# Row maxima of the attention scores: 1024 columns at a time from the operands that lie on all 128 rows

## The chip, the core and the metric

The kernel runs on one core of one Trainium2 chip. Each engine of the core (TensorE = PE, VectorE = DVE, ScalarE = ACT, GpSimd = POOL, SyncE = SP) works through its own list of instructions in order; semaphores are all that orders one engine against another. The metric is the time of one execution on the device in microseconds (us). In the profile PEld is TensorE's load of stationary weights, which runs beside its matmuls; L943 is line 943 of the kernel.

## The reference

One attention layer over 16 images of 1024 tokens and 512 channels, with 8 heads of 64 channels:

```python
xn = silu(group_norm(x, gn_scale, gn_offset))
q, k, v = split(einsum('bxyc,cd->bxyd', xn, w_qkv), 3)      # 8 heads of 64 channels each
sim = einsum('bhdi,bhdj->bhij', q * 64 ** -0.5, k)          # 1024 x 1024 per head
out = einsum('bhij,bhdj->bhid', softmax(sim), v)
out = einsum('bxyd,dc->bxyc', out, w_out) + b_out + x
```

## The kernel before

Matrix products run in fp16, but nearly all operands are split in a high half and a low half, so that a product is made of high x high, high x low and low x high.

**Steps and units.** An image takes four steps, one per pair of heads, and a step has 16 units. A unit `v` (`UNITS = 64` per image, 1024 in all) is 256 keys against 512 queries of one head. In each unit TensorE's list holds:

- `scores`: four matmuls of 512 columns into the PSUM tile ST (lines 1018 and 1019), which has two buffers;
- `times_v` of unit v - 2: eighteen small matmuls with V into PV (line 1052);
- one "side" task in most units, by the table `SIDE`: a projection of q or k ("qk") or of v ("v") for a later step, or the output projection ("out"), each 12 matmuls of 512 columns (line 929); or four fp32 transposes ("xt" line 992, "ot" line 986); or a small matmul for the group norm. All side tasks write the one-buffer PSUM tile SD.
- "tops", below.

ScalarE takes the exponential of each unit twice (lines 591 and 594, 128x1024 each). The low half Pl = P - Ph is made by VectorE for even units (`low_probs`, line 795) and by GpSimd for odd ones (line 492). In unit v VectorE drains the side task of unit v - 1; for "qk" and "v" ScalarE writes the high half first (line 553 or 558) and VectorE the low half after it (line 682 or 687). `times_v` of a unit waits for its exponentials and its Pl; `scores` of unit v waits for the exponentials of unit v - 2; a side task waits until the one before it is drained.

**Tops.** The softmax needs, before the scores of a head, a shift for each query: about the maximum of its row of scores. For one head this is 16 matmuls of 512 columns, for 8 blocks of 128 queries and 2 halves of the keys (line 943). Each takes the high half of q and of k of one head straight from the projections' result `QK_hi`, where a head lies on 64 of the 128 rows, and writes one of the two 512-column buffers of the PSUM tile TP. VectorE takes the maximum of each (line 741, `mx`). After four blocks VectorE joins the two halves (line 731) and makes `ms` (line 733), TensorE spreads `ms` over the rows with four 128-column matmuls (line 951), and VectorE copies that into the operand Q2 (line 746). `TOPS_PER_W` gives the number of tops in each of 8 successive units (3, 2, 3, 2, 3, 2, 2, 1), `TOP_PLACES` their places on TensorE around `times_v` and around and within the side task (a projection is cut in two parts of six matmuls), and `TOPS_AHEAD` their places on VectorE before or after `low_probs`.

**Placement.** `scores` contracts over 128 rows: K1 and Q1 hold, for one head, the high half of k and q on its 64 rows, and the low half of k with the high half of q on the other 64. K2 and Q2 hold the low half of q with the high half of k, and the shifts with a constant. SP builds the four from `QK_hi` and `QK_lo` by 12 DMAs per pair (`place`, line 385), put at unit 10 of the step before (`PLACE_AT`). SP's list also holds the loads of x for the next image (line 361; "xt" number t + 2 is loaded when number t has been transposed) and the loads and stores of the result.

Of the kernel before, what the change touches and what calls it, by code (L numbers as in the profile page):

```python
# [10 lines left out]
ALU = mybir.AluOpType  # L28
# [16 lines left out]
PLACED = 6 * 16  # L45
# [6 lines left out]
Q_SCALE, K_SCALE, V_SCALE = 3, 4, 5  # L52
DVE_STEPS = 7
TOPS_PER_W = [3, 2, 3, 2, 3, 2, 2, 1]
# [17 lines left out]
def head_tops(pair, hh):  # L72


    maxima = [("max", pair, hh, qb, kh) for qb in range(TB) for kh in range(2)]
    return maxima[:10] + [("shift", pair, hh, 0)] + maxima[10:] + [("shift", pair, hh, 1)]


def top_uses(step, u, last=False):


    w, hh = u % 8, u // 8
    if last and step == 3 and hh == 1:
        return []
    done = sum(TOPS_PER_W[:w])
    return head_tops(*((step, 1) if hh == 0 else ((step + 1) % 4, 0)))[done:done + TOPS_PER_W[w]]

TOPS_SINCE_SHIFT = (7, sum(TOPS_PER_W[:4]))

# [19 lines left out]
SPLIT = ("qk", "v", "out")  # L112
# [30 lines left out]
def follows_split(step, u, first=False, last=False):  # L143

    return any(use[0] in SPLIT for use in side_before(step, u, first, last))

# [10 lines left out]
def image_before(use, b, step, u):  # L157
# [4 lines left out]


# [3 lines left out]
            + [use for t in range(TB) for use in [("v", t)] + head_tops(0, 0)[9 * t // 4:9 * (t + 1) // 4]])  # L167
# [5 lines left out]
class Count:  # L173

    PER_IMAGE = {"side": len(IMAGE_USES), "hi": sum(x[0] in HI_PARTS for x in IMAGE_USES),
                 "top": HEADS * 18, "shifts": 2 * HEADS}

    def __init__(self, side=0, hi=0, top=0, shifts=0, mark=None):  # L180
# [959 lines left out]
```

## Time and profile before

| | |
|---|---|
| Median of 3 runs | 4224.94 us (4224.76 to 4225.04) |
| Time of the profiled execution | 4226.06 us |
| Its span, first to last instruction | 4224.3 us |
| Instructions | 94104 |
| PE busy | 3989.4 us (94%) |
| DVE busy | 3128.5 us (74%) |
| ACT busy | 2835.4 us (67%) |
| POOL busy | 1626.7 us (39%) |
| Mean granted TensorE clock | 0.981 of full speed |
| Largest shares of the chain that ended last | PE SD L929 31%, PE PV L1052 13%, PE TP L943 10%, PE ST L1018 and L1019 6% each |

A line of a timeline gives the start of an instruction, or of a merged run of like ones, and how long it lasted, in us, then engine, line, operation, and output <- inputs. Matmuls overlap: one of 512 columns lasts 0.38 us and the next of its kind starts about 0.215 us after it. So TensorE's cost is read from start to start. An inner image takes 256.0 us (between ScalarE's first exponentials of one image and of the next).

### The profile page before, as it was taken

Reading aid. Unit: us, or ns where it says so; the run is one execution under the profiler, and the core shown is the slowest. Engines: PE = TensorE matmul, PEld = TensorE weight load, DVE = VectorE, ACT = ScalarE, POOL = GpSimd, SP = SyncE. Lnnn points to the kernel's source line nnn. Section 1 sums busy time; section 2 is a strip of 40 time slices with the busy share of each in tenths; the row PEclk is TensorE's granted clock in tenths of the full one; section 3 lists DMA queues with packets and bytes.
Section 4 is the critical chain, followed back from the end, with each engine's and each line's share of the span. In section 5 each row is a group of like instructions: output and inputs, shape, how many; then the busy total and the mean of one; then the engine's idle time right before and its main releaser. Section 6 shows DMA issues by size and latency. Waiting matters only on the chain.

```text
span 4224.3 us, 94104 instructions
## 1 busy us (share of the span) xinstructions
PE 3989.4 (94%) x32844; PEld 2038.7 (48%) x32844; DVE 3128.5 (74%) x5216; ACT 2835.4 (67%) x3202; POOL 1626.7 (39%) x1226
## 2 busy tenths in 40 slices
PE   3899999999999999999999999999999999999997
PEld 1444545445454444545445454454544545454443
DVE  5686777868777687776877778687776877778774
ACT  2576676767667676676766767676676766767664
POOL 1243343433434343343433434333343433434333
PEclk8999999999999999999999999999999999999999
DMA  2111212122031120311112121220311203121121
GB/s 77 28 49 36 71 31 76 31 61 61 16 91 31 51 56 19 88 31 56 51 43 68 28 76 33 59 61 16 91 31 51 56 24 83 31 59 49 39 60 33
DMA packets 119394, 211.50 MB, mean 50 GB/s; under 512 B 19536, under 2 KB 19536, under 8 KB 118992
## 3 DMA queue, kind: packets, MB, share of 16 engines
q1 hardware_dynamic: 118992, 205.86, 18.0%
q8 instruction: 286, 4.69, 0.5%
q14 instruction: 116, 0.95, 0.1%
HBM read 71.57 MB, written 33.55 MB: 25 GB/s over the span
## 4 chain that ended last, share of the span: by engine, by line
PE 71%; issue 12%; DVE 9%; POOL 4%; ACT 3%; DVEq 1%; DMA 0%; SPq 0%; ACTq 0%; POOLq 0%
PE SD L929 31%; PE PV L1052 13%; PE TP L943 10%; PE ST L1018 6%; PE ST L1019 6%; DVE Pl L795 2%; DVE mx L741 2%; POOL Pl L492 2%; PE SD L992 1%; POOL xn L479 1%; PE TP L951 1%; ACT QK_hi L553 1%; PE SD L986 1%; ACT Ph L594 1%; DVE Q L746 1%
## 5 line engine op out<-in xcount | busy, mean ns | idle before, releaser
L741 DVE TENSOR_REDUCE mx<-TP 128x1 f32<-128x512 f32 x2048 | 1349.3, 684 | 346.7 <-PE TP L943 338.1
L591 ACT ACTIVATE P<-ST,cns 128x1024 f32<-128x1024 f32 x1024 | 1142.6, 1116 | 532.6 <-PE ST L1019 484.1
L492 POOL TENSOR_TENSOR Pl<-P,Ph 128x1024 f16<-128x1024 f32 x512 | 1116.6, 2181 | 796.2 <-ACT Ph L594 796.0
L594 ACT ACTIVATE Ph<-ST,cns 128x1024 f16<-128x1024 f32 x1024 | 1138.0, 1111 | 0.0
L1052 PE MATMUL PV<-V,Ph 128*128 128x129 f16 (+2 forms) x10240 | 884.9, 212 | 43.7 <-POOL Pl L492 31.0
L1052 PEld LDWEIGHTS PV<-V,Ph 128*128 128x128 f16 x10240 | 766.6, 98 | 309.4 <-issue 271.9
L1052 PE MATMUL PV<-V,Pl 128*128 128x65 f16 x8192 | 850.1, 194 | 0.0
L943 PE MATMUL TP<-QK_hi 64*128 64x512 f16 x2048 | 722.6, 388 | 70.8 <-DVE mx L741 50.0
L1018 PE MATMUL ST<-Q,K 128*128 128x512 f16 x2048 | 785.7, 384 | 1.8 <-issue 0.2
L1019 PE MATMUL ST<-Q,K 128*128 128x512 f16 x2048 | 785.0, 383 | 0.0
L929 PE MATMUL SD<-xn,wq 128*128 128x512 f16 x3072 | 735.9, 382 | 25.3 <-POOL xn L479 16.0
L1052 PEld LDWEIGHTS PV<-V,Pl 128*128 128x128 f16 x8192 | 732.5, 99 | 3.9
L499 POOL TENSOR_TENSOR O<-pv_sum,den 128x256 f32<-128x256 f32 x256 | 169.2, 661 | 1412.0 <-DVE pv_sum L803 1407.0
L795 DVE TENSOR_TENSOR Pl<-P,Ph 128x1024 f16<-128x1024 f32 x512 | 662.0, 1293 | 8.7 <-ACT Ph L594 8.7
L553 ACT ACTIVATE QK_hi<-SD,sc 128x512 f16<-128x512 f32 x256 | 175.9, 687 | 525.7 <-PE SD L929 525.7
L682 DVE SCALAR_TENSOR_TENSOR QK_lo<-SD,sc,QK_hi 128x512 f16<-128x512 f32 x256 | 192.2, 751 | 355.9 <-ACT QK_hi L553 340.1
L929 PEld LDWEIGHTS SD<-xn,wq 128*128 128x128 f16 x3072 | 269.7, 98 | 374.5 <-issue 83.5
L943 PEld LDWEIGHTS TP<-QK_hi 64*128 64x128 f16 x2048 | 159.7, 93 | 553.1 <-issue 290.8
L929 PE MATMUL SD<-wo,OT 128*128 128x512 f16 x1536 | 363.0, 381 | 16.4 <-DVE OT L694 10.4
L929 PE MATMUL SD<-wq,xn 128*128 128x512 f16 x1536 | 364.6, 381 | 10.8 <-DVE V L687 6.5
L1018 PEld LDWEIGHTS ST<-Q,K 128*128 128x128 f16 x2048 | 203.5, 99 | 213.6 <-issue 33.5
L1019 PEld LDWEIGHTS ST<-Q,K 128*128 128x128 f16 x2048 | 201.6, 98 | 184.6 <-issue 5.0
(92 smaller groups left out, 2826.3 us busy)
## 6 DMA issues: line engine op xcount, KB each, us to landing
work<-in_x SPq DMA_DIRECT2D x128, 256.0 KB, 2.7
Q<-QK_hi SPq DMA_DIRECT2D x256, 128.0 KB, 2.7
K<-QK_hi SPq DMA_DIRECT2D x256, 128.0 KB, 2.8
res<-in_x SPq DMA_DIRECT2D x128, 256.0 KB, 3.0
out<-res SPq DMA_DIRECT2D x128, 256.0 KB, 2.3
K<-QK_lo SPq DMA_DIRECT2D x128, 128.0 KB, 2.7
Q<-QK_lo SPq DMA_DIRECT2D x128, 128.0 KB, 2.7
V<-in_L_conv_w_qkv SPq DMA_DIRECT2D x1, 3072.0 KB, 10.4
```

Source lines behind the costliest of these rows:

```text
L492: nc.gpsimd.tensor_tensor(Pl[:, v % 4, :], P32[:, v % 2, :], Ph[:, v % 4, :], ALU.subtract).then_inc(lo_pool, 1)
L553: nc.scalar.activation(QK_hi[:, pair % 2, i, bass.ts(half, HALF)], SD[:], ACT.Identity, scale=sc[:, col:col + 1]).then_inc(side_hi, 1)
L591: nc.scalar.activation(P32[:, v % 2, :], ST[:, v % 2, :], ACT.Exp, scale=cns[:, 0:1])
L594: nc.scalar.activation(Ph[:, v % 4, :], ST[:, v % 2, :], ACT.Exp, scale=cns[:, 0:1]).then_inc(exp_done, 1)
L682: nc.vector.scalar_tensor_tensor(out=QK_lo[:, i, cols], in0=SD[:], scalar=sc[:, col:col + 1], in1=QK_hi[:, pair % 2, i, cols], op0=ALU.mul ...
L741: nc.vector.reduce_max(mx[:, hh, qb, kh:kh + 1], TP[:, cnt.top_bank], AX.X).then_inc(top_drained, 1)
L795: nc.vector.tensor_tensor(Pl[:, v % 4, :], P32[:, v % 2, :], Ph[:, v % 4, :], ALU.subtract).then_inc(lo_dve, 1)
L929: ins = nc.tensor.matmul(SD[:], stationary(i, c), moving(j, c), start=(c == 0 and i + j == 0), stop=(c == CC - 1 and i == 1))
L943: ins = nc.tensor.matmul(TP[:, bank], QK_hi[r, pair % 2, 0, bass.ts(qb, P)], QK_hi[r, pair % 2, 1, bass.ts(kh, HALF)], start=True, stop=True)
L1018: nc.tensor.matmul(dst, K1[:, slot, kb], Q1[:, slot, bass.ts(q, HALF)], start=True, stop=False)
L1019: ins = nc.tensor.matmul(dst, K2[:, slot, kb], Q2[:, slot, bass.ts(q, HALF)], start=False, stop=True)
L1052: ins = nc.tensor.matmul(PV[:, cols], stationary, moving, start=kb == qb == n == 0, stop=kb == TB - 1, skip_group_check=True)
```

## The change

The maxima are now formed from the operands that the DMAs have placed (q high against k high on a head's 64 rows, q high against k low on the other 64), one block of 128 queries in each unit: two matmuls of 512 columns into the two banks of TP, which is now one buffer of 1024 columns, and one `reduce_max` over 1024. They stand right behind `scores`; the shift matmuls stand at the end of their unit. A block's maxima are taken `TOP_LEAD` = 6 units before the scores of that block's place. On VectorE the order in a unit is: shift copy of the unit before, side task of the unit before, maximum, `low_probs`. The projections are no longer cut in two. q, k and their low halves lie in one buffer `QK` (without a second buffer of the high halves), `QK1` takes the place of Q1 and K1, `QK2` that of Q2 and K2, and a pair is placed by 6 DMAs of twice the size. They are put right behind the last "qk" of a step, at unit 5, 6, 7 and 5 of steps 0 to 3. TensorE's first maximum of a head waits for its placement (`placed`), which before only the scores waited for; this is at unit 10 of a step for the next pair.

```diff
-PLACED = 6 * 16
+PLACED = 3 * 16
+Q_HI, Q_LO, K_HI, K_LO = range(4)
-TOPS_PER_W = [3, 2, 3, 2, 3, 2, 2, 1]
+TOP_LEAD = 6
+def unit_max(step, u, last=False):
+    head, qb = divmod(16 * step + u + TOP_LEAD, TB)
+    return [] if last and head == HEADS else [("max", head // 2 % 4, head % 2, qb)]
+def unit_shift(step, u, last=False):
+    head, qb = divmod(16 * step + u + TOP_LEAD, TB)
+    if qb == 4 and not (last and head == HEADS):
+        return [("shift", head // 2 % 4, head % 2, 0)]
+    if qb == 0:
+        return [("shift", (head - 1) // 2, (head - 1) % 2, 1)]
+    return []
-TOPS_AHEAD = [[1, 0], [0, 0]]
-TOP_PLACES = [[(1, 2, 3), (2, 2, 3)], [(0, 1, 3), (1, 1, 3)]]
-PLACE_AT = 10
+PLACE_AT = [max(u for u, kind in units.items() if kind == "qk") for units in SIDE]
...
-        QK_hi = sb("QK_hi", [P, 2, 2, TOK], F16)
-        QK_lo = sb("QK_lo", [P, 2, TOK], F16)
-        K1 = sb("K1", [P, 4, TOK], F16)
...
+        QK = sb("QK", [P, 4, TOK], F16)
+        QK1 = sb("QK1", [P, 4, 2, TOK], F16)
+        QK2 = sb("QK2", [P, 4, 2, TOK], F16)
-        TP = ps("TP", [P, 2, 512], F32)
+        TP = ps("TP", [P, 2 * HALF], F32)
...  SP, place
-                    for dst, src in ((Q1[r, slot, :], q_hi), (K1[r, slot, :], k_hi),
-                                     (Q1[other, slot, :], q_hi), (K1[other, slot, :], QK_lo[r, 1, :]),
-                                     (Q2[r, slot, :], QK_lo[r, 0, :]), (K2[r, slot, :], k_hi)):
+                    for dst, src in ((QK1[r, slot], QK[r, Q_HI:4:K_HI - Q_HI]),
+                                     (QK1[other, slot], QK[r, Q_HI:4:K_LO - Q_HI]),
+                                     (QK2[r, slot], QK[r, Q_LO:K_HI + 1])):
                         sp.dma_start(dst, src).then_inc(placed[hh], 16)
...
-                    if u == PLACE_AT and not (last and s == 3):
+                    if u == PLACE_AT[s] and not (last and s == 3):
...  DVE, top_use and step
-                    nc.vector.reduce_max(mx[:, hh, qb, kh:kh + 1], TP[:, cnt.top_bank], AX.X
+                    nc.vector.reduce_max(mx[:, hh, qb:qb + 1], TP[:], AX.X).then_inc(top_drained, 1)
...
+                    for use in shift_before(s, u, last):
+                        top_use(use, cnt)
                     for use in side_before(s, u, first, last):
                         side(use, image_before(use, b, s, u), cnt)
-                    for use in tops[:ahead]:
+                    for use in unit_max(s, u, last):
                         top_use(use, cnt)
                     if v % 2 == 1:
                         low_probs(b, v - 1)
...  PE, top_use, scores and step
-                wait(pe, top_drained, cnt.top - 1)
+                wait(pe, top_drained, cnt.top)
-                    if qb == kh == 0:
-                        wait(pe, side_drained, cnt.mark["qk"])
-                    ins = nc.tensor.matmul(TP[:, bank], QK_hi[r, pair % 2, 0, bass.ts(qb, P)],
-                                           QK_hi[r, pair % 2, 1, bass.ts(kh, HALF)],
+                    if qb == 0:
+                        pe.wait_ge(placed[hh], PLACED * (4 * image + pair + 1))
+                    for kh in range(2):
+                        ins = nc.tensor.matmul(TP[:, bass.ts(kh, HALF)], QK1[:, slot, 0, bass.ts(qb, P)],
+                                               QK1[:, slot, 1, bass.ts(kh, HALF)], start=True, stop=True)
...
                     scores(b, v, 0, cnt)
                     scores(b, v, 1, cnt)
+                    for use in unit_max(s, u, last):
+                        top_use(use, image_of_tops(b, s, u), cnt)
                     if not (first and v < 2):
                         times_v(*before, 0, cnt)
                         times_v(*before, 1, cnt)
-                    for use in tops[place[0]:place[1]]:
...
+                    for use in side_uses(s, u, first, last):
+                        side(use, image_of(use, b, s), cnt)
+                    for use in unit_shift(s, u, last):
+                        top_use(use, image_of_tops(b, s, u), cnt)
```

TensorE, unit 0 of step 1 from its projection on, and the start of unit 1. Before:

```order
L929 MATMUL SD<-xn,wq 128x512 x6
L208 REGISTER_ALU
L943 MATMUL TP<-QK_hi 128x512
L929 MATMUL SD<-xn,wq 128x512 x6
L208 REGISTER_ALU
L1018 MATMUL ST<-Q,K 128x512
L1019 MATMUL ST<-Q,K 128x512
L1018 MATMUL ST<-Q,K 128x512
L1019 MATMUL ST<-Q,K 128x512
L208 REGISTER_ALU
L943 MATMUL TP<-QK_hi 128x512
```

And after the change:

```order
L891 MATMUL SD<-xn,wq 128x512 x12
L184 REGISTER_ALU
L970 MATMUL ST<-QK 128x512
L971 MATMUL ST<-QK 128x512
L970 MATMUL ST<-QK 128x512
L971 MATMUL ST<-QK 128x512
L184 REGISTER_ALU
L905 MATMUL TP<-QK 128x512 x2
```

The matmuls of the tops no longer stand inside the projection; two stand together behind the scores. REGISTER_ALU rows set the count for a wait. In the order before, 24 separate groups of L943 matmuls stand in each step, with matmuls over 128 rows on both sides of each; after, 16 groups of two.

VectorE, unit 1 of step 3: it drains the projection of unit 0 (L682), makes Pl of unit 0 (L795), takes maxima (L741) and handles the sums of the softmax (L802, L803). Before:

```order
L682 SCALAR_TENSOR_TENSOR QK_lo<-SD,sc,QK_hi 128x512
L792 REGISTER_ALU
L795 TENSOR_TENSOR Pl<-P,Ph 128x1024
L738 REGISTER_ALU
L741 TENSOR_REDUCE mx<-TP 128x1
L738 REGISTER_ALU
L741 TENSOR_REDUCE mx<-TP 128x1
L802 RECIPROCAL den<-pv_sum 128x4
L803 TENSOR_TENSOR pv_sum<-pv_sum 128x3x64
```

And after:

```order
L650 SCALAR_TENSOR_TENSOR QK<-SD,sc,QK 128x512
L704 REGISTER_ALU
L707 TENSOR_REDUCE mx<-TP 128x1
L699 TENSOR_SCALAR ms<-mx,cns 128x4
L757 REGISTER_ALU
L760 TENSOR_TENSOR Pl<-P,Ph 128x1024
L766 REGISTER_ALU
L767 RECIPROCAL den<-pv_sum 128x4
L768 TENSOR_TENSOR pv_sum<-pv_sum 128x3x64
```

The maximum, and in every fourth unit `ms` too, now stand ahead of Pl.

SP, second half of step 1: before, the last of the six loads of x stand ahead of the placement.

```order
L361 DMA work<-in_x 128x512
L208 REGISTER_ALU
L361 ISA
L361 DMA work<-in_x 128x512
L378 REGISTER_ALU
L385 DMA Q<-QK_hi 64x1024
```

And after:

```order
L330 DMA work<-in_x 128x512
L347 REGISTER_ALU
L353 DMA QK<-QK 64x2x1024 x2
L353 DMA QK<-QK 64x2048
L353 DMA QK<-QK 64x2x1024 x2
L353 DMA QK<-QK 64x2048
L184 REGISTER_ALU
L330 ISA
L330 DMA work<-in_x 128x512
```

The placement has moved ahead of the last three loads of x (the first of the three is shown).

## Rows read from the trace of the kernel before

**Rows 1.** The page, busy time of each engine over the whole span.

```profile
PE 3989.4 (94%) x32844; PEld 2038.7 (48%) x32844; DVE 3128.5 (74%) x5216; ACT 2835.4 (67%) x3202; POOL 1626.7 (39%) x1226
```

**Rows 2.** Busy time by stretch: step 0, 1, the halves of 2, and 3.

```profile
1394.30:1461.00 66.70, 65.92 (x537) 33.20 (x537) 46.70 (x76) 40.04 (x45) 26.48 (x16) 1.00 0.25 67
1461.00:1518.70 57.70, 57.51 (x505) 30.88 (x503) 44.60 (x73) 42.02 (x48) 18.42 (x12) 1.00 0.26 71
1518.70:1551.90 33.20, 31.44 (x260) 16.52 (x259) 25.91 (x57) 23.02 (x27) 14.23 (x19) 1.00 0.10 32
1551.90:1586.00 34.10, 30.16 (x237) 15.45 (x237) 30.60 (x48) 29.27 (x35) 16.34 (x12) 0.90 0.20 47
1586.00:1650.30 64.30, 62.73 (x517) 30.98 (x516) 45.34 (x74) 42.35 (x48) 25.80 (x17) 1.00 0.11 26
```

**Rows 3.** Timeline of TensorE's matmuls in two units of step 1.

```profile
1999.63 1.46 PE L929 MATMUL SD<-xn,wq 128*128 128x512 f16 x6
2000.93 0.38 PE L1018 MATMUL ST<-Q,K 128*128 128x512 f16 x1
...
2001.58 0.38 PE L1019 MATMUL ST<-Q,K 128*128 128x512 f16 x1
2001.79 0.39 PE L951 MATMUL TP<-ident,ms 128*128 128x128 f16 x4
2002.02 0.22 PE L1052 MATMUL PV<-V,Ph 128*128 128x129 f16 x1
...
2002.72 0.63 PE L992 MATMUL SD<-ident,work 128*128 128x128 f32 x4
2003.19 0.38 PE L1018 MATMUL ST<-Q,K 128*128 128x512 f16 x1
...
2003.84 0.38 PE L1019 MATMUL ST<-Q,K 128*128 128x512 f16 x1
2004.15 0.39 PE L943 MATMUL TP<-QK_hi 64*128 64x512 f16 x1
2004.47 0.23 PE L1052 MATMUL PV<-V,Ph 128*128 128x129 f16 x1
...
2005.28 0.60 PE L943 MATMUL TP<-QK_hi 64*128 64x512 f16 x2
2005.81 0.66 PE L992 MATMUL SD<-ident,work 128*128 128x128 f32 x4
```

**Rows 4.** Timeline of the other engines in the same stretch.

```profile
2001.13 0.69 ACT L553 ACTIVATE QK_hi<-SD,sc 128x512 f16<-128x512 f32 x1 [1.77 <-PE SD L929]
...
2001.85 0.75 DVE L682 SCALAR_TENSOR_TENSOR QK_lo<-SD,sc,QK_hi 128x512 f16<-128x512 f32 x1 [1.46 <-ACT QK_hi L553]
...
2001.99 1.11 ACT L591 ACTIVATE P<-ST,cns 128x1024 f32<-128x1024 f32 x1 [0.18 <-PE ST L1019]
...
2002.52 1.22 DVE L795 TENSOR_TENSOR Pl<-P,Ph 128x1024 f16<-128x1024 f32 x1
```

**Rows 5.** The page's groups: count, busy us, mean ns, idle before.

```profile
L741 DVE TENSOR_REDUCE mx<-TP 128x1 f32<-128x512 f32 x2048 | 1349.3, 684 | 346.7 <-PE TP L943 338.1
```

**Rows 6.** Timeline of DVE in the second half of step 2.

```profile
1560.52 1.87 DVE L741 TENSOR_REDUCE mx<-TP 128x1 f32<-128x512 f32 x3
...
1562.62 1.31 DVE L733 TENSOR_SCALAR ms<-mx,cns 128x4 f16<-128x4 f32 x1
```

**Rows 7.** Timeline of ACT in the same half step.

```profile
1564.00 1.11 ACT L591 ACTIVATE P<-ST,cns 128x1024 f32<-128x1024 f32 x1 [1.35 <-POOL Pl L492]
...
1573.57 0.69 ACT L558 ACTIVATE V<-SD,sc 128x512 f16<-128x512 f32 x1 [2.05 <-PE SD L929]
```

**Rows 8.** Timeline of SP's DMA issues in step 1.

```profile
1498.50 0.59 SPq L385 DMA_DIRECT2D K<-QK_hi  x1
1499.14 0.59 SPq L385 DMA_DIRECT2D Q<-QK_hi  x1
```

**Rows 9.** The page's DMA issues: count, KB each, median us to landing.

```profile
work<-in_x SPq DMA_DIRECT2D x128, 256.0 KB, 2.7
```

More of the change, by code:

```diff
@@ L69, in v_slot, with shift_before @@
     return head + 4 if head < 4 else head - 4
[L72 to L91, printed above, removed]
+def unit_max(step, u, last=False):
[8 more added lines that the diff above has]
+    return []
+def shift_before(step, u, last=False):
+    if u > 0:
+        return unit_shift(step, u - 1, last)
+    return unit_shift(step - 1, 15, last) if step > 0 else []
 SIDE = [
@@ L140, in side_before, with image_of_tops @@
     return side_uses(step - 1, 15, first, last) if step > 0 else []
-def follows_split(step, u, first=False, last=False):
-    return any(use[0] in SPLIT for use in side_before(step, u, first, last))
+def image_of_tops(b, step, u):
+    return b + (16 * step + u + TOP_LEAD) // (8 * HEADS)
 def image_of(use, b, step):
@@ L549, in side @@
                     _, pair, which, half = use
-                    wait_placed(act, 4 * image + pair - 1)
-                    i, col = (0, Q_SCALE) if which == "q" else (1, K_SCALE)
-                    nc.scalar.activation(QK_hi[:, pair % 2, i, bass.ts(half, HALF)], SD[:], ACT.Identity,
+                    wait_placed(act, 4 * image + pair)
+                    hi, col = (Q_HI, Q_SCALE) if which == "q" else (K_HI, K_SCALE)
+                    nc.scalar.activation(QK[:, hi, bass.ts(half, HALF)], SD[:], ACT.Identity,
                                          scale=sc[:, col:col + 1]).then_inc(side_hi, 1)
@@ L814, in step @@
                     v = 16 * s + u
+                    for use in shift_before(s, u, last):
+                        top_use(use, cnt)
                     for use in side_before(s, u, first, last):
                         side(use, image_before(use, b, s, u), cnt)
-                    tops = top_uses(s, u, last)
-                    late = follows_split(s, u, first, last)
-                    ahead = TOPS_AHEAD[u % 8 == 7][late]
-                    for use in tops[:ahead]:
+                    for use in unit_max(s, u, last):
                         top_use(use, cnt)
@@ L823, in step @@
                         low_probs(b, v - 1)
-                    for use in tops[ahead:]:
-                        top_use(use, cnt)
                     if v % 4 == 1 and not (first and v == 1):
@@ L954, in top_use, with side @@
                 cnt.passed(use)
-            def side(use, image, cnt, part=None):
+            def side(use, image, cnt):
                 kind = use[0]
-                if part != 1:
-                    wait(pe, side_drained, cnt.side)
-                if kind in ("qk", "v") and part != 1:
+                wait(pe, side_drained, cnt.side)
+                if kind in ("qk", "v"):
                     half = use[3] if kind == "qk" else use[1] // 4
@@ L1059, in step @@
                     v = 16 * s + u
-                    sides, tops = side_uses(s, u, first, last), top_uses(s, u, last)
                     before = (b, v - 2) if v >= 2 else (b - 1, UNITS + v - 2)
@@ L1063, in step @@
                     scores(b, v, 1, cnt)
-                    late = follows_split(s, u, first, last)
-                    place = TOP_PLACES[u % 8 == 7][late]
-                    for use in tops[:place[0]]:
-                        top_use(use, cnt)
+                    for use in unit_max(s, u, last):
+                        top_use(use, image_of_tops(b, s, u), cnt)
                     if not (first and v < 2):
```

92 lines of the change are left out of this document (33 added, 59 removed).

## The prediction

> **What bounds the kernel now.** I read the busy times first: PE 94%, DVE 74%, ACT 67%, POOL 39% [rows 1]. An engine at 94% is the bound almost everywhere, so the first question is what TensorE's time consists of, and the second where it waits. Cut by steps, one inner image takes 66.7 + 57.7 + 67.3 + 64.3 = 256.0 us [rows 2]. Only in step 2 is PE clearly less than full (31.4 of 33.2 us, then 30.2 of 34.1, at a granted clock of 0.90); there ACT is at 29.3 and DVE at 30.6 of 34.1.
>
> A busy PE is not yet a PE at its peak, so I read its timeline from start to start [rows 3]. Scores: 2000.93 to 2001.79 = 0.86 us for four matmuls, 0.215 each. A projection: six matmuls in 1999.63 to 2000.93 = 1.30, thus 2.59 for twelve. Shift matmuls 0.23. `times_v` 2002.02 to 2002.72 = 0.70. Four fp32 transposes 0.47. Now the tops. From the last score matmul to the shift's first, both over 128 rows, it is 0.21 us (2001.58 to 2001.79). From the last score matmul to a maximum matmul over 64 rows it is 0.31 (2003.84 to 2004.15), and from there back to 128 rows 0.32 (2004.15 to 2004.47), where 0.215 is what 512 columns take. A run of two takes 0.53 up to the next 128-row matmul instead of 0.43 (2005.28 to 2005.81). So each change of the row count costs 0.10 us, each group of tops 0.20. This hides inside the busy time, since the matmul before is still ending. It is not the semaphore wait: the shift matmuls have one too and pay nothing.
>
> There are 24 such groups in a step: 4.8 us a step, 19.2 an image, 307 us in 16 images.
>
> Check of this reading. Without tops' changes of rows a unit costs PE 0.86 (scores) + 0.43 (two maximum matmuls) + 0.70 (`times_v`) = 1.99 us, and on top 2.59 for a projection, 0.47 for transposes, 0.23 for a shift (4 a step). By SIDE the steps have 10, 6, 7 and 9 projections and 4, 8, 2 and 2 transposes: 60.5, 52.0, 52.1 (with 0.3 for the two small matmuls) and 57.0 us. With 4.8 each: 65.3, 56.8, 56.9, 61.8 = 240.8. Measured 66.7, 57.7, 67.3, 64.3. So real waits are only 1.4, 0.9, 10.4 and 2.5 = 15.2 us an image. The three parts of an image are 221.6 of streaming, 19.2 of row changes, 15.2 of waits.
>
> **The change part by part.**
>
> *Maxima over 128 rows.* As many matmuls of as many columns as before (1024 x 2), but between neighbours of 128 rows. They then cost 0.215 us each, like the scores beside them: -19.2 us an image. The bounds: no gain at all if the 0.10 us belongs to a change of output tile (against it stands the shift's 0.21), and -19.2. I take -19.2.
>
> The Trainium skill ("TensorE: Matmul & The Clock Gate", section on packing small matmuls) speaks against this: a weight load runs beside matmuls in flight only when its row group differs. By that rule 128-row loads would not hide, and 2048 loads of 0.1 us would give back about 200 us. The trace of this case does not bear it out: score matmuls over 128 rows, each with a load of its own, follow one another in 0.215 us [rows 3]. The same skill's "TensorEngine Tiling (Array Packing)" (key properties) says that a change of the tiling mode drains the array; that is what the 0.10 us looks like. By the first rule the forecast would be about 4215 us.
>
> *One reduce of 1024 for two of 512.* One of 512 takes 0.684 us [rows 5], three in a row 1.87 [rows 6], so 0.6 from start to start. One of 1024 is bounded by 1.37 (2 x 0.684) above and 1.2 (2 x 0.6) below; a DVE operation of 1024 in this trace takes 1.22 [rows 4], and I take that. DVE saves some 60 us and a small reduce (41 us in all) for each shift. DVE is not the bound outside step 2, so I count nothing for this by itself.
>
> *One TP buffer, new order: the new waits.* Here the forecast is decided. I lay out one pair of units by the intervals of the rows. When TensorE goes on from a projection to the next unit (2000.93 in [rows 3]), ACT starts the high half 0.20 us later, and DVE makes the low half from 0.92 to 1.67 us [rows 4]. An even unit with "qk", then a light odd one, times from the odd unit's start: PE fills the maximum by 1.4; DVE ends the low half at 1.6, the maximum at 2.8, and only then makes Pl of the even unit, done at 4.0. `times_v` for that Pl stands in the next unit, at 1.99 + 1.29 = 3.3 (3.75 if the odd unit has transposes). That is a wait of 0.3 to 0.7 us, where before Pl came first and no wait showed. In every fourth unit (v mod 4 = 1) `ms` stands between, which takes 0.5 to 1.3 us [rows 6]: the wait becomes 1.0 to 1.5. Units with a projection themselves (4.6 us) hide all of it. The one buffer costs little: the next maximum matmul comes a unit later, 2 us at least against 1.22. Only a shift at the end of a light unit waits 0.6 to 0.9 for the maximum (unit 6 of step 3). Adding by SIDE:
> - step 0: light odd units 1, 3, 9, 11, of which 1 and 9 with `ms`: 2.7 us.
> - step 1: units 1, 3, 5, 9, 15: 2.8, and 2.5 from the placement, below.
> - step 3: units 1, 3, 6 and 7, 9, 11: 4.4.
> - step 2, first half: mostly projections, 1.5 over its 27.7 of streaming: 29.2 against 33.2. Second half: ACT sets the pace. Its work is 29.3 [rows 2]; its largest waits now are 1.35 behind GpSimd's Pl and 2.05 behind PE [rows 7], after three maxima in one unit [rows 6], which no longer occur. I take 31.8 against 34.1 (between 29.3 and 34.1, the low clock may stay).
>
> *Placement.* 6 DMAs of 256 KB instead of 12 of 128. SP issues one every 0.64 us [rows 8]. If a double one takes as long, the six take 3.8 us, if double as long 7.7; landing comes 2.7 us after the issue, by the loads of x of the same size [rows 9]. Two things can be late. (a) Unit 10's first maximum waits for the first three: the shortest time is in step 1, where 0.86 + three units of 2.46 = 8.2 us lie between the start of unit 7 and this matmul, against 1.7 (drain) + 1.3 to 2.6 + 2.7 = 5.7 to 7.0. It is in time, by a little. Step 2 has about as much (its units 8 and 9 take 3.4 us on ACT). (b) The load of x for "xt" 5 stands behind the placement on SP: issued at 1.7 + 3.8 = 5.5, landed at 8.2 (up to 12.1), where PE wants it at 2 x 2.46 + 1.99 = 6.9. Before it was issued ahead of the placement and nothing waited. So 1.3 to 5.2 us once an image, nearer to the first; I take 2.5. Transfers beside each other could add to it.
>
> *Sum.* Streaming 221.6; waits 2.7 + 5.3 + (29.2 + 31.8 - 52.1 = 8.9) + 4.4 = 21.3; together 242.9 us an image, by 15.2 - 21.3 + 19.2 = 13.1 less than 256.0. First and last image have a few units less: 15.75 x 13.1 = 206 us. The prologue has 16 groups with row changes (3.2 us) and five top matmuls fewer ahead of the loop; with its wait for the placement I count 4 us. The profiled execution took 4226.06 us for a span of 4224.3: 4226 - 210 = 4016. The median lies 1.1 us lower: **4015 us**.
>
> **The rivals.**
> - *The waits stay as they were* (best case), 15.2 us an image: all 19.2 are gained, -19.2 x 15.75 - 4 = -306: 3920 us. For it: DVE has slack of a quarter of the span. Against it: Pl moves behind a maximum on an in-order engine.
> - *New waits eat most of it*: twice the 12.4 us that I count outside step 2, and step 2 stays at 65: 259 would be a loss; with 1.5 times and 65 it is 169.5 + 18.6 + 65 = 253, or -3 x 15.75 - 4 = -51: 4175 us.
> - *Slower, by one mechanism*: Pl for even units, behind the maximum and `ms` on DVE, becomes TensorE's bound. Price: the eight odd units of a step would each hold `times_v` by 0.8 us or more: 6.4 a step against 4.8 saved, +1.6 x 63 = +100: 4325 us. It decides from 0.6 us a unit (4.8 / 8). Against it: four or more of the eight odd units hold a projection or follow one that leaves 2.6 us of cover.
> - *The 0.10 us isn't the row change* but goes with every group: 24 groups become 16, -1.6 a step or -100, and my new waits of 6 an image give +95: about 4220 us, no change. Against it is the shift's 0.21 [rows 3].
>
> **How the numbers follow.** The forecast 0.61 (its own range 3960 to 4080), the best case 0.20, most of it eaten 0.12, slower 0.04, groups 0.03. Of the eaten case nearly all is still faster. What a measurement of this kernel can tell from no change is 0.2%, 8.4 us. Faster: 0.61 + 0.20 + 0.11 = 0.92; same 0.03; slower 0.05. The range for 8 in 10 takes in the best case and the worse half of my own waits: 3910 to 4090.
>
> **What would show it.** In the trace after: maximum matmuls start 0.215 us behind the last score matmul, and PV 0.43 behind the first of them; if it is 0.31 and 0.53, the first step is wrong. The reduces take near 1.22 us. PE waits for DVE's Pl at `times_v` behind light odd units, for `mx` at shifts, and once an image for a load of x in step 1; without these step 0 is under 62 us. Step 1 should hardly gain (57.3), steps 0 and 3 some 3 us each, step 2 about 6. The forecast fails low if DVE catches up within a unit, and high if the low clock spreads as PE waits more.

## The result: slower, and where an image spends its time now

The changed kernel takes 4330.3 us (4329.4 to 4331.1, 4 runs) against 4225.0 (4224.8 to 4225.9): ratio 1.0249, 95% interval 1.0231 to 1.0267. The forecast was 4015 us, with a range of 3910 to 4090. The result is slower than the kernel before and outside the range, and it came about in another way than the slower rival's.

The page of the changed kernel gives the busy time of each engine. It answers [rows 1].

```profile
PE 3827.5 (88%) x32844; PEld 2133.3 (49%) x32844; DVE 3022.1 (70%) x3936; ACT 2851.5 (66%) x3202; POOL 1717.7 (40%) x1226
```

PE's busy time fell by 162 us, while the span grew by 104. So the time in which PE is idle grew by 266 us, from 235 to 501. The mean granted clock fell from 0.981 to 0.958: TensorE spent 362 us at its lower level (1.2 GHz) instead of 160. Score matmuls start 0.43 us apart at that level and 0.215 at the higher one, so these 202 us more are at most 101 us of time lost (an estimate: half of them, if all of it was work).

Windows of an inner image, cut as in [rows 2]: step 0, step 1, the halves of step 2, step 3. After the busy times come the granted clock, the DMA engines' busy share and GB/s.

```profile
1429.14:1496.62 67.48, 62.17 (x536) 34.44 (x537) 45.74 (x55) 40.36 (x44) 27.03 (x16) 1.00 0.24 67
1496.62:1559.36 62.74, 56.85 (x506) 33.23 (x504) 40.98 (x53) 42.35 (x49) 20.81 (x14) 0.95 0.24 64
1559.36:1594.08 34.72, 30.70 (x260) 17.38 (x261) 26.76 (x47) 22.84 (x26) 14.87 (x19) 0.95 0.10 31
1594.08:1629.24 35.16, 29.21 (x238) 15.95 (x236) 31.79 (x39) 29.37 (x35) 16.79 (x12) 0.85 0.20 46
1629.24:1691.94 62.70, 59.08 (x516) 32.28 (x516) 41.51 (x54) 42.82 (x47) 27.73 (x18) 1.00 0.12 26
```

Over the inner images (medians) the steps go from 66.7, 57.7, 67.3, 64.3 to 67.5, 62.8, 69.8, 62.7: 256.0 to 262.8 us. Steps 1 and 2 carry the loss (5.1 and 2.5 us), step 0 lost 0.8, and step 3 gained 1.6. Step 1's clock was 1.00 before and is 0.95 now.

**The row changes are gone, as forecast.** TensorE's matmuls of two units of step 1, answering [rows 3]:

```profile
1496.12 0.38 PE L971 MATMUL ST<-QK 128*128 128x512 f16 x1
1496.34 0.59 PE L905 MATMUL TP<-QK 128*128 128x512 f16 x2
1496.77 0.22 PE L1004 MATMUL PV<-V,Ph 128*128 128x129 f16 x1
...
1503.54 0.59 PE L905 MATMUL TP<-QK 128*128 128x512 f16 x2
1504.73 0.23 PE L1004 MATMUL PV<-V,Ph 128*128 128x129 f16 x1 [0.60 <-DVE Pl L760]
```

From the last score to the maximum it is 0.22 us (0.31 before), from the two maximum matmuls to `times_v` 0.43 (0.53 before). Each of these loads its own 128 rows of weights, and still no time for the load shows. The Trainium skill's rule on packing small matmuls ("TensorE: Matmul & The Clock Gate"), that a load overlaps matmuls only when its row group differs, does not hold here if it is taken by itself. The same section also lets a load into a background weight buffer go ahead, and that would agree with the trace; no run here shows which buffer is used. The last line is the first of the new waits.

The waits of TensorE over the whole run: us in total, times, longest.

```profile
PE PV L1004 <- DVE Pl L760: 122.8, 217, 1.2
PE SD L947 <- DMA work<-in_x: 90.5, 20, 16.0
PE TP L905 <- DVE QK L711: 53.8, 46, 2.0
PE TP L912 <- DVE mx L707: 53.7, 70, 2.3
PE SD L891 <- DVE OT L662: 45.3, 16, 2.9
PE TP L905 <- DMA QK<-QK: 42.6, 16, 2.9
```

Of these lines the first, the fourth and, in part, the second were forecast; the longest wait of the second, 16.0 us, is the first load of the whole run. The fifth and sixth come once an image, the third about three times, and they were not forecast. The page's groups put them beside the work, and answer [rows 5] and [rows 9] (the last line: KB each, median us to landing):

```profile
L707 DVE TENSOR_REDUCE mx<-TP 128x1 f32<-128x1024 f32 x1024 | 1248.3, 1219 | 234.0 <-PE TP L905 223.8
L905 PE MATMUL TP<-QK 128*128 128x512 f16 x2048 | 640.6, 396 | 105.4 <-DVE QK L711 53.8
...
QK<-QK SPq DMA_DIRECT2D x384, 256.0 KB, 4.8
work<-in_x SPq DMA_DIRECT2D x128, 256.0 KB, 2.8
```

The reduce takes 1.22 us, as assumed. The placement's DMA lands 4.8 us after its issue, where I had taken 2.7 from a load of x of the same size.

**Wait 1, step 1.** First SP's issues in the timeline, then the time from issue to landing of the first of the three loads of x behind the copies (`--source L330` in the window 1531:1532), then TensorE:

```profile
1525.02 5.91 SPq L353 DMA_DIRECT2D QK<-QK  x6
1531.18 5.81 SPq L330 DMA_DIRECT2D work<-in_x  x3
```

```profile
DMA to landing us min/median/max: 4.1/4.1/4.1
```

```profile
1535.40 1.08 PE L947 MATMUL SD<-ident,work 128*128 128x128 f32 x4 [4.61 <-DMA work<-in_x]
1536.28 0.63 PE L970 MATMUL ST<-QK 128*128 128x512 f16 x1
1536.70 0.63 PE L971 MATMUL ST<-QK 128*128 128x512 f16 x1
...
1540.96 0.39 PE L912 MATMUL TP<-ident,ms 128*128 128x128 f16 x4
1541.18 0.38 PE L970 MATMUL ST<-QK 128*128 128x512 f16 x1
```

Six issues fill SP for 5.9 us. The first three take 0.60 to 0.72 us each (medians), like those of 128 KB in [rows 8]; the last three take 1.2 to 1.3. Only then is the load of x issued, 6.2 us after the first copy, where I had counted 3.8. It lands 4.1 us later, where I had counted 2.7: the loads of x with no copies ahead of them land after 2.6 to 2.8 us. TensorE waits 4.6 us. Its granted clock falls to the lower level in this wait, at 1534.0, and stays there until 1540.9: the score matmuls start 0.43 us apart instead of 0.215. The stretch from 1535.40 to 1540.96 holds some 3 us of work at the higher level. So this wait costs about 7 us an image (4.6 and 2.6), not 2.5.

**Wait 2, step 2.** SP, then TensorE:

```profile
1594.64 5.96 SPq L353 DMA_DIRECT2D QK<-QK  x6
```

```profile
1597.60 0.38 PE L971 MATMUL ST<-QK 128*128 128x512 f16 x1
1600.69 0.61 PE L905 MATMUL TP<-QK 128*128 128x512 f16 x2 [2.71 <-DMA QK<-QK]
```

The three DMAs of the first head are in place 6.0 us after the first issue, where the forecast had 4.0 to 5.3. TensorE is ready for this maximum at 1597.98, only 3.3 us after that issue. From the start of unit 8 (1592.94) to there it is 5.0 us, because units 8 and 9 took TensorE 2.0 us each; the forecast had given them ScalarE's 3.4 us each and had called step 2 "about as much" as step 1's 8.2. With 5.0 us, even its own 5.7 us for drain and placement would have been late.

**Wait 3, step 0.** VectorE, GpSimd and TensorE around the copy of V:

```profile
1458.65 1.22 DVE L760 TENSOR_TENSOR Pl<-P,Ph 128x1024 f16<-128x1024 f32 x1
1459.78 3.17 DVE L775 COPY V<-V 128x4160 f16<-128x4160 f16 x1
1462.87 0.68 DVE L662 TENSOR_TENSOR OT<-SD,OT 128x512 f16<-128x512 f32 x1
```

```profile
1459.18 2.67 POOL L460 TENSOR_TENSOR Pl<-P,Ph 128x1024 f16<-128x1024 f32 x1 [3.31 <-ACT Ph L562]
```

```profile
1463.69 2.75 PE L891 MATMUL SD<-wo,OT 128*128 128x512 f16 x12 [2.89 <-DVE OT L662]
```

The same pair in the kernel before, VectorE and then GpSimd:

```profile
1423.92 1.22 DVE L795 TENSOR_TENSOR Pl<-P,Ph 128x1024 f16<-128x1024 f32 x1
1425.05 0.68 DVE L746 CAST Q<-TP 64x512 f16<-64x512 f32 x1
1425.65 1.23 DVE L810 COPY V<-V 128x4160 f16<-128x4160 f16 x1
```

```profile
1425.47 3.39 POOL L492 TENSOR_TENSOR Pl<-P,Ph 128x1024 f16<-128x1024 f32 x1 [3.62 <-ACT Ph L594]
```

In both kernels the copy meets GpSimd's low half, and one of the two stands until the other is nearly done. Before, GpSimd stood (3.39 us; alone it takes 2.12) and TensorE had cover for it. Now VectorE stands, 3.17 us for a copy of 1.22, and the projection behind it waits 2.9 us. In all 16 images it is so; the copy's durations (min, median, max, ns), before and after:

```profile
L810 DVE COPY V<-V x16: 1224/1225/1226, 160.9 to 3988.8; 128x4160 f16<-128x4160 f16 x16
```

```profile
L775 DVE COPY V<-V x16: 3167/3170/3172, 157.6 to 4089.5; 128x4160 f16<-128x4160 f16 x16
```

The Trainium skill has the rule ("SBUF — State Buffer", section "SBUF: two separate sides"): VectorE, in a two-port mode or with two inputs in SBUF, and GpSimd share one pair of ports as an exclusive lock; whichever starts first has it for the whole instruction, and the other blocks. The trace agrees on the blocking: the copy ends 1.10 us after GpSimd's low half (1462.95 and 1461.85), about its own 1.22. It does not show that the first to start wins: in the kernel before the low half's record begins 0.18 us ahead of the copy's (1425.47 and 1425.65), and GpSimd stood all the same. What decides is open here.

**Wait 4, first half of step 2.** The same meeting in a chain of small operations, VectorE and then TensorE (GpSimd's low half ran from 1585.55 for 2.12 us):

```profile
1585.57 2.13 DVE L737 TENSOR_TENSOR gn<-gn 128x4 f32<-128x4 f32 x1
1587.73 0.16 DVE L739 TENSOR_TENSOR gn<-bet,gn 128x4 f32<-128x4 f32 x1
...
1588.47 0.68 DVE L711 CAST QK<-TP 64x512 f16<-64x512 f32 x1
```

```profile
1589.20 0.60 PE L905 MATMUL TP<-QK 128*128 128x512 f16 x2 [1.82 <-DVE QK L711]
```

An operation on four columns takes 2.13 us, the cast of the shift stands behind it, and the cast alone frees the one TP buffer for the next maximum. The meeting as such is not new. In the kernel before the same operation took as long:

```profile
L772 DVE TENSOR_TENSOR gn<-gn x16: 161/1979/1984, 56.7 to 3853.2; 128x4 f32<-128x4 f32 x16
```

There TensorE waited 0.3 us in this half for the shift's copy; now it is 1.8.

### The profile page after: what moved, and what is told of

Its sections match the earlier page's. It is cut to its first block, busy times and chain, and to the rows that moved or that the text cites. A ratio compares the mean times of both kernels' runs of the same rounds, so it can differ in the third digit from the quotient of the medians.

```text
span 4328.5 us, 90413 instructions
## 1 busy us (share of the span) xinstructions
PE 3827.5 (88%) x32844; PEld 2133.3 (49%) x32844; DVE 3022.1 (70%) x3936; ACT 2851.5 (66%) x3202; POOL 1717.7 (40%) x1226
## 4 chain that ended last, share of the span: by engine, by line
PE 52%; DVE 19%; issue 16%; ACT 4%; POOL 4%; SPq 2%; DMA 2%; DVEq 1%; POOLq 0%; ACTq 0%
PE SD L891 27%; PE PV L1004 9%; DVE Pl L760 5%; DVE mx L707 5%; PE TP L905 5%; PE ST L971 4%; PE ST L970 4%; POOL Pl L460 3%; SPq L353 2%; DVE work L750 2%; ACT QK L521 2%; DMA work<-in_x 1%; PE TP L912 1%; ACT Ph L562 1%; PE SD L947 1%
## 5 line engine op out<-in xcount | busy, mean ns | idle before, releaser
L460 POOL TENSOR_TENSOR Pl<-P,Ph 128x1024 f16<-128x1024 f32 x512 | 1212.0, 2367 | 920.4 <-ACT Ph L562 917.3
L707 DVE TENSOR_REDUCE mx<-TP 128x1 f32<-128x1024 f32 x1024 | 1248.3, 1219 | 234.0 <-PE TP L905 223.8
L1004 PE MATMUL PV<-V,Ph 128*128 128x129 f16 (+2 forms) x10240 | 893.7, 213 | 133.9 <-DVE Pl L760 122.8
L970 PE MATMUL ST<-QK 128*128 128x512 f16 x2048 | 807.3, 394 | 0.4
L971 PE MATMUL ST<-QK 128*128 128x512 f16 x2048 | 807.1, 394 | 0.0
L905 PE MATMUL TP<-QK 128*128 128x512 f16 x2048 | 640.6, 396 | 105.4 <-DVE QK L711 53.8
L891 PE MATMUL SD<-xn,wq 128*128 128x512 f16 x3072 | 707.1, 380 | 21.8 <-POOL xn L447 16.0
L650 DVE SCALAR_TENSOR_TENSOR QK<-SD,sc,QK 128x512 f16<-128x512 f32 x256 | 191.7, 749 | 369.4 <-ACT QK L521 333.0
L521 ACT ACTIVATE QK<-SD,sc 128x512 f16<-128x512 f32 x256 | 175.9, 687 | 399.9 <-PE SD L891 399.9
L711 DVE CAST QK<-TP 64x512 f16<-64x512 f32 x256 | 175.9, 687 | 342.5 <-PE TP L912 342.1
L905 PEld LDWEIGHTS TP<-QK 128*128 128x128 f16 x2048 | 177.4, 100 | 430.0 <-DVE QK L711 165.4
L970 PEld LDWEIGHTS ST<-QK 128*128 128x128 f16 x2048 | 207.4, 101 | 171.3 <-issue 18.0
## 6 DMA issues: line engine op xcount, KB each, us to landing
QK<-QK SPq DMA_DIRECT2D x384, 256.0 KB, 4.8
work<-in_x SPq DMA_DIRECT2D x128, 256.0 KB, 2.8
res<-in_x SPq DMA_DIRECT2D x128, 256.0 KB, 2.8
out<-res SPq DMA_DIRECT2D x128, 256.0 KB, 2.0
bias<-in_L_conv_b_out SPq DMA_DIRECT2D x1, 256.0 KB, 7.4
```

Of the source, the lines that this page charges most:

```text
L460: nc.gpsimd.tensor_tensor(Pl[:, v % 4, :], P32[:, v % 2, :], Ph[:, v % 4, :], ALU.subtract).then_inc(lo_pool, 1)
L521: nc.scalar.activation(QK[:, hi, bass.ts(half, HALF)], SD[:], ACT.Identity, scale=sc[:, col:col + 1]).then_inc(side_hi, 1)
L650: nc.vector.scalar_tensor_tensor(out=QK[:, lo, cols], in0=SD[:], scalar=sc[:, col:col + 1], in1=QK[:, hi, cols], op0=ALU.mult, op1=ALU.sub ...
L707: nc.vector.reduce_max(mx[:, hh, qb:qb + 1], TP[:], AX.X).then_inc(top_drained, 1)
L891: ins = nc.tensor.matmul(SD[:], stationary(i, c), moving(j, c), start=(c == 0 and i + j == 0), stop=(c == CC - 1 and i == 1))
L905: ins = nc.tensor.matmul(TP[:, bass.ts(kh, HALF)], QK1[:, slot, 0, bass.ts(qb, P)], QK1[:, slot, 1, bass.ts(kh, HALF)], start=True, stop=True)
```

## The experiments

Image and step times are medians over the inner images of the profiled run.

**Is the 0.10 us the row change?** The kernel before, with only the rows of the maximum matmul changed:

```
-ins = nc.tensor.matmul(TP[:, bank], QK_hi[r, pair % 2, 0, bass.ts(qb, P)],
-                       QK_hi[r, pair % 2, 1, bass.ts(kh, HALF)], ...
+ins = nc.tensor.matmul(TP[:, bank], QK_hi[:, pair % 2, 0, bass.ts(qb, P)],
+                       QK_hi[:, pair % 2, 1, bass.ts(kh, HALF)], ...
```

The maxima are then those of the sum of two heads' scores. That is not the maximum of the head whose scores are shifted, so this version serves to measure time and leaves out the right shift.

> The kernel before, with one edit: the matmuls of the maxima contract over all 128 rows of QK_hi, both heads of the pair, instead of one head's 64; order, buffers and reduces stay. The maxima are those of the sum of two heads' scores, so the output isn't the reference's. Theory (a change of the row count costs 0.10 us, 24 groups a step): each group loses 0.20 us, 19.2 us an image, 307 us in all, less what returns as waits on VectorE, which has 0.3 us less for each group: 3925 to 4000 us. Rival (the 0.10 us goes with a change of the output tile or the semaphore, not the rows): 4225 us.

Measured 4060.1 us (4058.9 to 4064.6), ratio 0.9606 (0.959 to 0.9622). The row change is the 0.10 us, and taking it out alone wins 165 us. By the count of groups it is 307 us of TensorE's time, and PE's busy time fell by 277. The rest went into waits: what an image takes beyond streaming and row changes grew from 15.2 to 24.0 us, and TensorE's waits for VectorE's maxima alone from 50.0 to 81.7 us in the run. The steps take 63.6, 54.7, 66.7 and 60.6 us: three are shorter by 3.0 to 3.7 us, step 2 only by 0.6, since TensorE does not bound it. TensorE also spent 44 us less at the lower clock, which is up to 22 of the 165 us.

**And the other way round:** the changed kernel, maxima over the head's 64 rows of the same tiles (`QK1[rows_of(hh), slot, ...]`).

> The changed kernel, with one edit: the matmuls of the maxima contract over the head's own 64 rows of QK1 (the same products as in the kernel before). Theory: 16 groups a step pay 0.20 us again, of which about a third falls into waits that are there anyway: 4330 + 130 to 200 = 4460 to 4530 us. Rival (row count costs nothing): 4330 us.

Measured 4382.9 us, ratio 1.037 (1.0353 to 1.0388): 53 us more, not 130 to 200. The size was missed: PE's busy time rose by 136 us, and more than half of it fell where TensorE waits anyway. Its waits for Pl are 71.5 us in this run, 122.8 without the row changes.

**The placement.** The second head's three DMAs are issued at unit 11, behind the loads of x:

```
 if u == PLACE_AT[s] and not (last and s == 3):
-    place((s + 1) % 4, cnt)
+    place((s + 1) % 4, cnt, (0,))
+if u == 11 and not (last and s == 3):
+    place((s + 1) % 4, cnt, (1,))
```

> The changed kernel, but only the first head's three DMAs stand right behind the last q/k projection; the second head's three stand at unit 11, behind the loads of x. Theory (the load of x behind six placement DMAs costs step 1 4.9 us and then some 2.4 us at the low clock): 5 to 7 us an image go, -80 to -110: 4220 to 4250 us; step 2's wait for the first head's placement stays. Rival (the step is limited by VectorE's chain, the wait only moves): 4310 to 4330 us.

Measured 4236.7 us (4230.1 to 4241.5), ratio 1.0025 (1.0015 to 1.0034): 94 us less, as theory 1 said. Step 1 in this kernel, to be read beside the second window above:

```profile
1461.61:1518.72 57.11, 54.40 (x506) 31.53 (x504) 40.99 (x53) 42.24 (x49) 20.80 (x14) 1.00 0.27 71
```

Step 1 goes from 62.7 to 57.1 us, the clock is back at 1.00, and PE is busy 2.5 us less for the same matmuls: that is the part of the price that was the lower clock. The wait for x is 1.2 us instead of 4.6. That step 1 now stands at the forecast's 57.3 is chance, since those 57.3 held 2.5 us for this wait and 2.8 for Pl (here 1.2 and 1.9). The first half of step 2 also fell, from 34.7 to 33.2 us, with its clock at 1.00 instead of 0.95. The wait for the placement in step 2 stays (42.1 us in 16 waits).

**The copy of V** at unit 13 of step 0 instead of 7 (`if s == 0 and u == 13: move_v(b, cnt)`).

> The changed kernel with one edit: VectorE's copy of V (line 775, once an image) stands at unit 13 of step 0 instead of unit 7. In the changed kernel it takes 3.17 us (1.22 before) beside GpSimd's Pl, and the output projection of unit 8 starts 3.06 us late behind it (0.86 before). Theory: the wait at unit 8 goes and unit 13 has slack: -2 to -3 us an image, 4285 to 4300 us. Rival (the wait is that of the transposes' own chain over ScalarE): 4325 to 4335 us.

Measured 4275.9 us, ratio 1.0116 (1.0099 to 1.0133): 54 us less, somewhat more than expected. The wait went (step 0 takes 64.5 us), and nothing came in its place.

**Both together.**

> The changed kernel with the second head's three DMAs at unit 11 and the copy of V at unit 13 of step 0. Theory 1 (the two waits lie in different steps and add up): 4330 - 94 - 54 = 4182 us, 4165 to 4200. Theory 2 (an earlier image stage only moves the wait to the next thing that is late): 4215 us or more.

Measured 4178.3 us (4173.4 to 4179.6), ratio 0.9887 (0.987 to 0.9903): the two waits add up. Here the copy met nobody:

```profile
L777 DVE COPY V<-V x16: 1233/1238/1240, 173.8 to 3962.9; 128x4160 f16<-128x4160 f16 x16
```

With two things put elsewhere the change is a gain of 1.1%.

**Does the copy cost in any kernel?** The kernel before with maxima over 128 rows, and the copy at unit 13.

> The kernel before with maxima over all 128 rows, and the copy of V at unit 13 of step 0. Theory 1 (the copy costs TensorE time only where it runs beside GpSimd's low half, which it does not in the kernel before, where it takes 1.22 us): no change from 4060 us, within 10 us. Theory 2 (the copy costs where it stands at unit 7 in any kernel): 4010 to 4045 us.

Measured 4043.1 us (4042.6 to 4044.3), ratio 0.9569 (0.9553 to 0.9585), 17 us less than without the copy's move: theory 2's number. Theory 1 also had a wrong premise, since in the kernel before the copy does run beside the low half, and GpSimd stands. The copy's own time is the same in both (1.22 and 1.23 us). Step 0 gave 1.0 us an image, and the trace of the version without the move shows where it was:

```profile
1377.05 1.46 PE L929 MATMUL SD<-wo,OT 128*128 128x512 f16 x6 [0.90 <-DVE OT L694]
```

This output projection of unit 8 waits 0.9 us for VectorE, in whose list the copy stands ahead of OT; with the copy moved the wait is gone. So, as an estimate, a third of what the copy cost in the changed kernel (3.1 us an image) is its place in VectorE's list, and the rest is its standing behind GpSimd. This is the fastest version of the study, but, as said, with maxima that aren't the head's own.

**VectorE's new order.** Pl of the even unit ahead of the maximum, as it was before the change:

```
-for use in unit_max(s, u, last):
-    top_use(use, cnt)
 if v % 2 == 1:
     low_probs(b, v - 1)
+for use in unit_max(s, u, last):
+    top_use(use, cnt)
```

> The changed kernel with one edit: in odd units VectorE makes Pl of the unit before ahead of the maximum instead of behind it. Theory 1 (order alone holds times_v): the waits for Pl, 11.3 us an image, go: below 4220 us. Theory 2 (with one TP buffer the next unit's maximum matmul then waits for the late reduce in the same place, so the wait changes its name): 4300 to 4360 us. I hold the second.

Measured 4329.4 us, ratio 1.0247 (1.023 to 1.0264): no change. The waits of TensorE show why:

```profile
PE TP L905 <- DVE mx L707: 167.8, 272, 2.7
...
PE PV L1004 <- DVE Pl L760: 0.2, 1, 0.2
```

The wait for Pl is gone, and one for the TP buffer stands in its place. In a light unit with a Pl, VectorE has 2.4 us of maximum and Pl to do, TensorE 2.0. By steps it is not the same kernel: step 0 takes 69.8 us (67.5 before this edit) and step 2 66.3 (69.8), and the two nearly cancel.

**Two TP buffers of 512 and two reduces**, the rest as changed.

```
-    nc.vector.reduce_max(mx[:, hh, qb:qb + 1], TP[:], AX.X) ...
+    nc.vector.reduce_max(mx[:, hh, qb, kh:kh + 1], TP[:, cnt.top_bank], AX.X) ...
```

> The changed kernel with TP as two buffers of 512 columns again: in each unit two matmuls over 128 rows, each with its own wait, and two reduces of 512; the places stay. VectorE has 0.06 us more in each unit and the small reduce of the halves again. Theory (the single buffer costs the waits before a shift, 3.6 us an image, and part of those before a maximum outside the placement's): -3 to -5 us an image, and +1 for VectorE's longer chain: 4265 to 4310 us. Rival 1 (one reduce of 1024 is what keeps VectorE's chain short): slower, 4345 to 4400 us. Rival 2 (the single buffer is the main cause of the loss): below 4230 us.

Measured 4328.0 us, ratio 1.024 (1.0223 to 1.0257): no change, and none of the three forecasts came true. Two effects cancel: TensorE's waits before a shift fell from 53.7 to 16.9 us, those for Pl rose from 122.8 to 159.0. The run changes the width of the reduce and the number of buffers together, so it does not price either alone. The wait behind the cast of the shift (wait 4) stays, 58.1 us against 53.8, so a second buffer of 512 does not remove it.

**GpSimd makes the even units' low halves, VectorE the odd ones'**, so that VectorE's Pl stands in the even units, most of which have a projection on TensorE.

```
-if v % 2 == 1:                                  # VectorE
+if v % 2 == 0 and not (first and v == 0):
     low_probs(b, v - 1)
-if v % 2 == 0 and not (first and v == 0):       # GpSimd
+if v % 2 == 1:
     low_probs(b, v - 1)
```

> The changed kernel with the parities of Pl exchanged: GpSimd makes Pl of even units, VectorE of odd ones, so that VectorE's Pl stands in the even units, most of which have a projection on TensorE behind it. Theory (Pl behind a maximum in a light odd unit holds times_v, 11.3 us an image): most of it goes, -7 to -11 us an image: 4155 to 4220 us. Rival (one TP buffer and the length of VectorE's chain hold TensorE whatever the order): 4300 to 4350 us.

Measured 4265.4 us, ratio 1.0089 (1.0068 to 1.011): 65 us less, not 110 to 175. Steps 0, 1 and 3 gained (63.0, 61.2 and 59.7 us), but the first half of step 2 went from 34.7 to 41.8.

**All four edits.**

> The changed kernel with four edits together: second head placed at unit 11, parities of Pl exchanged, copy of V at unit 13, two TP buffers. By the sum of the parts (measured -94 and -65 us, expected -35 and -40): 4330 - 234 = 4096 us. If step 2's waits at the low clock come from the exchanged parities and the placement together, they are less than the sum: 4060 to 4100. Rival (the parts remove the same wait twice): above 4150 us.

Measured 4170.0 us (4164.6 to 4170.6), ratio 0.9862 (0.9845 to 0.9878). That is 74 us above the sum of 4096 that was expected. With all four gains as measured alone (94, 65, 54 and 2 us) the sum would be 4115, missed by 55: 2.3 us an image in step 2 and 1.0 in step 0. GpSimd in the first half of step 2:

```profile
1519.04 2.98 POOL L468 TENSOR_TENSOR Pl<-P,Ph 128x1024 f16<-128x1024 f32 x1 [8.72 <-ACT Ph L569]
1524.40 0.62 POOL L475 TENSOR_TENSOR O<-pv_sum,den 128x256 f32<-128x256 f32 x1 [2.39 <-DVE pv_sum L777]
1524.98 0.20 POOL L442 TENSOR_TENSOR nt<-gn 128x4 f32<-128x4 f32 x1
```

The twelve Newton steps, for which the coefficients of the next image wait, begin behind the low half and behind the sums.

**Is it GpSimd's queue or the shared port?** The same kernel, with the Newton steps ahead of that unit's low half.

> The version with all four edits, in which GpSimd runs its Newton steps at unit 5 of step 2 ahead of that unit's low half instead of behind it. Theory 1 (what makes the first half of step 2 last 40.7 us is GpSimd's queue: the Newton steps stand behind a low half): that half falls to 37 us or less and the time from 4170 to 4100 to 4125 us. Theory 2 (it is VectorE and GpSimd slowing each other, whatever the order in the queue): the half stays above 39.5 us, 4150 to 4190 us.

Measured 4117.6 us (4113.2 to 4119.8), ratio 0.9742 (0.9725 to 0.9758); the half takes 36.5 us, where it took 40.7. It was the queue: theory 1. GpSimd in this kernel, where the window of the half begins at 1483.11:

```profile
1505.28 0.20 POOL L442 TENSOR_TENSOR nt<-gn 128x4 f32<-128x4 f32 x1 [11.62 <-DVE gn L697]
```

The first Newton step starts 22.2 us into the step instead of 25.3 (1524.98 less 1499.73), as soon as VectorE has its input ready.

**The exchange outside step 2 alone**, with the placement and the copy moved.

```
+def low_on_dve(v):
+    v = v % 64
+    return (v % 2 == 1) != (v // 16 == 2)
...
```

> The same two edits, and GpSimd makes the low halves of the even units in steps 0, 1 and 3 alone; step 2 keeps the changed kernel's assignment. Theory 1 (the exchange costs only where GpSimd also carries the Newton steps and the low halves of the image): steps 0, 1 and 3 lose the 9 us per image that they lost with the exchange everywhere, of which some 3 were the copy's, so 4182 less 100 = 4080 us, 4050 to 4125, and the first half of step 2 stays under 37 us. Theory 2 (the exchange collides in every step): 4150 us or more.

Measured 4107.5 us (4105.5 to 4110.4), ratio 0.9724 (0.9707 to 0.974). The steps take 62.8, 55.9, 69.8 and 60.2 us. Theory 1 holds, in its range, and the first half of step 2 is 34.7 us. It is the fastest form of the change as made, with one buffer and 1024 columns. The kernel before with nothing but 128-row maxima stays ahead of it by 47 us (4060.1), and with the copy moved too by 64 (4043.1), but both take maxima that aren't the head's own.

## Why the prediction was wrong, step by step

- *Bound, and row changes at 19.2 us an image*: right. The starts in the trace after show it, and the first experiment shows it without any other part of the change.
- *The reduce of 1024 at 1.22 us*: right.
- *New waits for Pl behind the maximum*: right in place and in sum. From the starts of TensorE's instructions they are 3.5, 1.9 and 3.8 us in steps 0, 1 and 3, and 0.9 for the shift, where 2.7, 2.8 and 4.4 (with the shift) were laid out; step 2 adds 1.3. Units with `ms` wait 0.8 to 1.1, less than the 1.0 to 1.5 laid out. But undoing them alone (the order of Pl) gained nothing.
- *Placement, (b)*: the largest failed step that an experiment isolates. "Landed at 8.2 (up to 12.1) ... I take 2.5" became a landing at 11.8, a wait of 4.6 to 4.9 and the lower clock behind it. The mechanism was named and the wait lies inside its stated 1.3 to 5.2; the size was taken too near the lower end. The load of x that TensorE waits for is issued 6.2 us after the first copy instead of 3.8, since six copies in a row hold up SP's issues, and lands 4.1 us after its issue instead of 2.7. The copies themselves, 64 rows to 64 rows within SBUF, land 1.2 to 1.5 us apart, the first after 3.1, the last after 9.5 to 10.1. The clock had no price at all. Moving half of the placement was worth 94 us.
- *Placement, (a)*: "in time, by a little" failed in step 2: 2.7 us late in nearly every image. TensorE reached the maximum 5.0 us after the start of unit 8, not some 8, and the first three copies took 6.0 us instead of 4.0 to 5.3. The trace before held a better price than the loads of x: there the six copies of 128 KB for the first head were in place 5.7 us after the first issue (median). This was read from the trace; an earlier start was not tried.
- *Step 0*: 63.2 forecast, 67.5 measured. The copy of V meeting GpSimd was no term of the sum; moving the copy gave 3.1 us an image back, 54 in all. I priced VectorE's work by durations and never asked what GpSimd does in the same microseconds.
- *Step 2, 29.2 + 31.8*: measured 34.7 + 35.1, the largest miss of the four steps. I took "mostly projections" for TensorE being able to fill the first half. The experiment on 128 rows alone shows that half stays at 32.3 with nothing else changed; TensorE's waits there are behind VectorE, 2.0 us of them for maxima. In the changed kernel they are 1.8 us behind the cast of the shift (wait 4), 1.0 for Pl and 0.8 for `mx`, and 1.5 us of the half went with the lower clock when the placement was split. That the chain of the normalisation's coefficients is what holds the cast was read from the trace, not shown by a run. The second half holds the late placement and runs at a clock of 0.85.
- *The low clock "may stay"*: it spread from 160 to 362 us, at most 101 us of time by the estimate above. The text named this as the way to fail high, and gave it no price.

By steps the miss of 19.9 us an image (262.8 for 242.9) is 4.3 + 5.5 + 8.8 + 1.3. Of step 0's 4.3 moving the copy gives back 3.1, and splitting the placement gives back all of step 1's 5.5 and 1.6 of step 2's 8.8: these are shown by experiments that took the cause away. Of the rest of step 2 the late placement (2.7 to 2.9) and the chain are read from the trace, and only GpSimd's queue was tested, in another version. That part stays open.

The rivals: "slower, by one mechanism" gave nearly the right time (4325) by luck, for the wrong reason. Its price, 0.8 us on each of eight units a step, did not occur: 217 waits for Pl in the whole run, not 512.

## What to carry to other kernels

Where an engine is 94% busy, time taken out of it does not all become time won: a bit over half did (165 of 307 us), and only where nothing else in the edit moved. Price a moved DMA by one of its own kind (same memories, same rows, as many in a row), and look at what is queued behind it. Look at the granted clock behind a wait on TensorE too: behind the 4.6 us of step 1 and the 2.7 us of step 2 it was at the lower level, behind the 2.9 us of step 0 it was not. And when VectorE's order changes, lay GpSimd's timeline beside it: the same two SBUF operations, met 0.6 us into GpSimd's instead of 0.2, left the other engine standing.

## What the runs showed of the hardware that was not expected

- A VectorE operation on SBUF that meets GpSimd's low half can stand for nearly all the rest of it: 1.22 to 3.17 us for the copy, 0.16 to 2.13 for one on four columns. Or GpSimd stands: 2.12 to 3.39 us beside the copy in the kernel before. Reduces and casts from PSUM kept their times beside it: all 1024 reduces of the changed kernel took 1.20 to 1.23 us and all casts of the shift 0.67 to 0.70, with a low half running or without.
- Copies within SBUF of 256 KB in 64 rows, one behind the other, land every 1.2 to 1.5 us, some 200 GB/s. SP issues the first three in 0.60 to 0.72 us each, as at 128 KB (0.60), and the next three in 1.2 to 1.3.
- In the 4.6 us wait of step 1 TensorE's clock fell to 1.2 GHz and stayed there for 6.8 us, 5.4 of them behind the wait; the wait of 2.9 us in step 0 had nothing of the kind.
